# A four-layer block on one core: the first feed-forward's squares move from POOL to ACT, with new instruction orders and PSUM banks

## The reference

```
scores = q k^T + rope(q) rope(k)^T, causal softmax, 16 heads, then W_o      # attention
h = bitlinear(x, w_fc) + gate * (x @ v.T @ fast_b.T @ u.T)                  # first feed-forward
r = maximum(h, 0);  out = bitlinear(r * r, w_proj)
z = x @ W_in; conv; p_w = exp(..); sums = cumsum(p_w * cos / sin(phi)); silu; W_out   # mixer
h = relu(x @ W1 + b1);  out = h @ W2 + b2                                   # second feed-forward
```

## Time and profile before

| | |
|---|---|
| median of 3 runs | 1388.17 us (1387.15 to 1388.91) |
| the profiled execution | 1383.91 us |
| its span | 1382.1 us |
| mean granted clock of TensorE | 0.946 of full speed |
| batches' fc stage (first rectifier to last), of batches 1 to 7 | from 268.7, 437.1, 589.2, 743.7, 890.6, 1048.4, 1185.4 us |

### The profile page before, as it was taken

How to read it: one execution, slowest core, us unless ns; L and a number is a source line. 1 busy time by engine, 2 the same in 40 slices (tenths; PEclk the granted TensorE clock), 3 DMA queues, 4 the chain that set the end, 5 groups by cost and what they waited for, 6 DMA issues and landing times.

```text
span 1382.1 us, 23204 instructions
## 1 busy us (share of the span) xinstructions
PE 1194.7 (86%) x8060; PEld 775.0 (56%) x8060; DVE 1103.5 (80%) x2259; ACT 1054.4 (76%) x2111; POOL 346.8 (25%) x317
## 2 busy tenths in 40 slices
PE   4788995889899989899899999999999998782867
PEld 2575663466556755566656765675655765451434
DVE  2694278999688888989798998899799988988930
ACT  4575699868967998699967989698959887547532
POOL 2953202520133203221134101530133101401021
PEclk9799997999999999999999999999999999896879
DMA  7511341315133104512334131613252131013000
GB/s 235 123 25 36 85 132 41 101 37 140 47 77 90 34 19 145 123 31 54 111 78 98 24 110 39 145 24 96 69 105 57 24 125 31 30 51 105 16 16 16
DMA packets 72084, 101.65 MB, mean 74 GB/s; under 512 B 10640, under 2 KB 44064, under 8 KB 71968
## 3 DMA queue, kind: packets, MB, share of 16 engines
q1 hardware_dynamic: 71968, 100.16, 27.7%
HBM read 74.44 MB, written 25.69 MB: 72 GB/s over the span
## 4 chain that ended last, share of the span: by engine, by line
PE 37%; ACT 23%; DVE 22%; issue 9%; POOL 5%; DMA 2%; SPq 1%; DVEq 0%; POOLq 0%; ACTq 0%
PE ps L885 12%; PE ps L894 10%; DVE work L1526 7%; PE ps L968 4%; ACT work L1213 4%; ACT xnd L1156 3%; DVE work L1449 3%; PE ps L986 3%; ACT work L1220 3%; PE ps L1053 2%; PE ps L960 2%; DVE work L1517 2%; ACT work L1280 2%; POOL later_norms L764 2%; DVE work L1535 2%
## 5 line engine op out<-in xcount | busy, mean ns | idle before, releaser
L1526 DVE TENSOR_TENSOR_SCAN work<-work 128x512 f32<-128x512 f32 x256 | 318.5, 1278 | 38.5 <-ACT work L1280 35.7
L1213 ACT ACTIVATE work<-work 128x384 f32<-128x384 f32 (+3 forms) x512 | 266.4, 564 | 46.0 <-DVE work L1449 45.1
L764 POOL TENSOR_TENSOR later_norms<-later_norms,singles 128x2 f32<-128x2 f32 x112 | 100.8, 903 | 689.4 <-ACT xnd L1156 387.0
L1449 DVE CUSTOM_DVE_ANT_0 work<-ps,work 128x384 f32<-128x384 f32 (+3 forms) x512 | 223.6, 484 | 49.7 <-PE ps L960 47.3
L968 PE MATMUL ps<-ident,work 128*128 128x128 f32 x1280 | 198.9, 280 | 26.8 <-ACT work L1213 21.1
L968 PEld LDWEIGHTS ps<-ident,work 128*128 128x128 f32 x1280 | 149.7, 144 | 76.9 <-issue 51.2
L1220 ACT COPY work<-ps 128x512 f32<-128x512 f32 x300 | 172.0, 580 | 0.4 <-PE ps L968 0.2
L1535 DVE TENSOR_TENSOR work<-work 128x1024 f32<-128x1024 f32 x128 | 162.4, 1269 | 5.1 <-DVEq L1373 0.2
L960 PE MATMUL ps<-work 96*128 96x384 bf16 (+3 forms) x512 | 123.1, 307 | 10.9 <-DMA work<-scratch 8.3
L894 PE MATMUL ps<-wpr,hid 128*128 128x256 f32 x512 | 119.7, 393 | 10.4 <-POOL hid L784 10.4
L894 PE MATMUL ps<-wf,hid 128*128 128x256 f32 x512 | 119.3, 395 | 4.4 <-ACT hid L1296 3.6
(11 more groups left out here) (177 smaller groups left out, 1934.9 us busy)
## 6 DMA issues: line engine op xcount, KB each, us to landing
work<-values SPq DMA_DIRECT2D x64, 256.0 KB, 3.5
work<-ratios SPq DMA_DIRECT2D x64, 256.0 KB, 3.1
scratch<-work SPq DMA_DIRECT2D x32, 384.0 KB, 4.7
work<-scratch SPq DMA_DIRECT2D x64, 192.0 KB, 3.9
work<-scratch SPq DMA_DIRECT2D x64, 128.0 KB, 4.2
x_in<-x SPq DMA_DIRECT2D x8, 512.0 KB, 7.0
work<-scratch SPq DMA_DIRECT2D x64, 64.0 KB, 4.4
values<-work SPq DMA_DIRECT2D x16, 256.0 KB, 2.4
```

Of the source, the lines that this page charges most:

```text
L764: g_.tensor_tensor(rstds[chain][:, tokens], spreads[chain][:, tokens], power[:, tokens], ALU.pow).then_inc(*rstd.one)
L1213: i = s_.activation(part_of, part_of, ACT.Exp, scale=-1.0, bias=nmax[:, row:row + 1])
L1449: i = v_.tensor_tensor_reduce(sc[:, n % 4, at:at + nk], out_of(b, name)[:, at:at + nk], base_of(qt), -SCORE_SCALE, BIG, ALU.add, ALU.min, ...
L1526: v_.tensor_tensor_scan(ring[:, at, m, :], pwr[:, slot, :], ring[:, at, m, :], 0.0, ALU.mult, ALU.add).then_inc(*scanned.one)
```

## The change

ACT takes the squares, one tile behind its rectifier: after rectifying tile n it squares tile n-1, and after the last one both 6 and 7. POOL's item is gone. The signals are the same ones: the square waits for the rectifier's drained signal and gives `hid_sq`.

```diff
     "act": "ystats fstats fystats zstats oystats gstats gystats centre norm ... fc znorm ...",
-    "pool": "stats q k ystats fstats fc fystats zstats oystats gstats gystats gsum ternary tables late",
+    "pool": "stats q k ystats fstats fystats zstats oystats gstats gystats gsum ternary tables late",
...
@@ POOL
-                if item == "fc":
-                    is_drained(pool, b, f"fc{n}")
-                    g_.tensor_tensor(hid[:, n, :], hid[:, n, :], hid[:, n, :], ALU.mult).then_inc(*hid_sq.one)
...
@@ ACT
                     is_filled(act, b, f"fc{n}")
                     s_.activation(hid[:, n, :], out_of(b, f"fc{n}"), ACT.Relu, bias=zero[:, 0:1]
                                   ).then_inc(*drains(b, f"fc{n}"))
+                    for g in (n - 1, n) if n == HC - 1 else (n - 1,) if n else ():
+                        is_drained(act, b, f"fc{g}")
+                        s_.activation(hid[:, g, :], hid[:, g, :], ACT.Square).then_inc(*hid_sq.one)
...
@@ MERGE, all five strings, and BANKS: replaced. The first line of PE's:
-        "a2 p a4 p a3 p2 a p a p a27 p a3 p a4 p a26 p a p a11 p2 a13 p a p a7 p a19 d a2 d2 a4 d6 a3 d a9 d a2 "
+        "a8 p2 a6 p4 a58 p2 a2 p2 a p3 a12 p a15 p a2 p a19 d a2 d9 a3 d a5 d a6 d a2 d2 a13 d a5 d3 a6 d a5 d "
```

More of the change, by code:

```diff
@@ L174 @@
     "pe":
[10 rows of a table removed]
-    "act":
[15 rows of a table removed]
-    "dve":
[12 rows of a table removed]
[10 rows of a table added]
+    "act":
[14 rows of a table added]
+    "dve":
[12 rows of a table added]
     "pool":
-        "a p a4 p4 a4 d2 a3 d15 a4 d2 a3 d16 a7 d18 a d2 a d a2 d a3 d18 a d4 a5 d a d17 a d4 a3 d2 a3 d20 a7 d22 "
-        "a2 d34 p4",
[2 rows of a table added]
     "sp":
-        "a13 d2 a m4 d3 m13 a7 d3 m2 d m6 d m5 a3 m a2 m2 d m d a2 d3 m4 d m d m8 a3 m a2 m3 d2 a2 d2 m4 d2 m4 d "
-        "m5 a m a4 m3 d2 a2 d2 m4 d2 m6 d m5 a3 m a2 d m d a2 d4 m8 d m5 a2 m a3 m2 d m d a2 d2 m4 d2 m5 d m7 d m "
-        "d4 m4 d2 m13 d4",
[3 rows of a table added]
 }
 BANKS = """
-0123450123450132450132450132401534025430243502435124035241324512435214302154321042310234120345201342
@@ L226 @@
-0352430152431502674315607423516074235160742310546372051364253041625301764520376512750261754206152765
-4306153143405413025140365241064735106423514206351435120647351206437512064315042675140263542310643201
-3674103675146021546270516742503614570321673417023672146210356274130754137217267672054371620543715204
-3715204372470163457123406752346503742653071243061753672601536123065241653425145342731532417365402164
-5106754106237514062713450627467146702134567213456712345076123457103625413240652134025617306134270534
@@ L231 @@
-6754203752340715243712540672471562047512463720134572630517263405172065341720653406517240651740625173
-4506241735604723105742130752341065302176375401741645067541602576405170165307165326017365412763570256
-4710265473210546731246053124312640531264035712640532714562703146724036743126034571632470562752740652
-4602653746507314620436710432760134520714635016257306241536213651730462517304516270541267054167253014
-6725036210735612075316450312476052465740237064372160327106316034516304125364207641205436105736412057
@@ L236 @@
-612340576123057612430576123457623104576210453762104537621045
+0123450123450134250134250134201532045203420532405124305241024512405214035214052345203542053421530425
+3415234015230145672301465723014657203145720341705624175036470615370416523462135476251764205741062751
+6375640123670246137042167542306417230651726530172651726304517236107425361042576021456731504365104635
+1423051624056237052634072536024175602341750312547301531247603152743561273045230630512734605124730512
+4730521473051423574620371654371253647213452607145615201462543026573257013562751637215672165302761504
@@ new lines @@
+3201374201563724015246370152407152407631524572631547321567430215673402561342051463254351673562401674
+2410367210367250623570165206471062457106472135460371326507132465071436250714362145307214215307415320
+7645310726435176024136217042761054732604237143632716437163402164327147643170613740657142305647125703
+6125703612405617324017562401240715624071562430715642013647513720176051365270341642573140653431604531
+0543671520731625470126507215674023514603725407216547203157253761540327603152476032547036254307563214
@@ L237 @@
+5602753160732651736215340217365403645230642504326103564130510352710532607512034621057632516324507163
+254701632547163254071632547063245710632471065324710635247106
 """
```

## The result

The changed kernel takes 1390.28 us in the median of 12 runs (1389.13 to 1391.93); the kernel before, on the same chip, 1387.14 us. The ratio is 1.003, with a 95% interval of 1.0021 to 1.004: slower by 0.3%, some 4 us. The forecast was 6 us faster. The time lies inside the range, the sign is wrong.

A forecast was written before the change was run, and what follows sets the result against it. PE was taken as nearest to the bound, 93% busy in the middle, no engine filling the span. Terms -4.9 - 3.5 - 4.0 + 7.0 + 1.3 - 2.0 = -6.1 us, from 1388.17 to 1382.1 us; range 1369 to 1397.

The forecast's parts named there:

- batch 7's fproj: Batch 7's fc stage: without POOL's squares fproj can start at 1198.0, not 1202.93, 4.9 us earlier.
- batch 1's fproj: Batch 1's fc stage: squares end at 284.7 in place of 288.35; taken as 3.5 us earlier.
- middle, POOL's squares gone: Batches 2 to 6: DVE gains 8 us without POOL's squares, half of it on the path, 4 us (0 to 13).
- middle, ACT's cost: Batches 2 to 6: 40 squares put 23.6 us on ACT; between nothing and 14.5 us shown, 7 us taken.
- tables, with start and loads: The start's gain of 2 us and the two added table loads' cost of 1.3 us, together -0.7.
- the rest of the tables: Five orders and all banks differ over the whole middle; not priced, 6 us allowed either way.
- the two loads: ACT has 43 table loads in place of 41, 1.28 us each; half of 2.6 us shown, 1.3 us cost.
- all stayed in the fc stages: Batches 2 to 6: if ACT's squares all stayed in the fc stages, 14.5 us would show.
- ACT becomes the bound beside attention: Rival, 0.26: squares delay exps and transposes; all 23.6 us and both table loads show, +11.8, 1400 us.
- The squares are hidden in full: Rival, 0.18: ACT's idle time takes all the middle's squares, the 7 us fall away, -13.1, 1375 us.
- Gain and cost cancel: Rival, 0.16: about 14 of 26 us show, or the new order loses 6 us elsewhere; within 2.8 us of 1388.17.
- the start: Program start: DVE's constants' operation meets less of POOL's subtraction; 2 us gained of PE's 3.4 idle (0 to 3.4).

The follow-up runs named there:

- old_order_act: The kernel before with its orders and banks kept and all squares moved from POOL to ACT; ratio 1.0009 to the kernel before.
- new_order_pool: The changed kernel's orders and banks with the squares left on POOL; 21.5 us slower than the kernel before.
- experiment 3: Kernel before's orders, each POOL square replaced by two constant writes to the tile, without reading SBUF; ratio 0.9875 to the kernel before, 1366.37 us.

## Why the prediction was wrong

By its steps, in us, with what the runs put in their place. There are two ways from the kernel before to the kernel after, and they give the steps different sizes: move the squares in the old tables and then change the tables, or change the tables first and then move the squares.

```
                              taken    squares moved first    tables changed first
batch 7's fproj               -4.9     -5.0                   -4.2
batch 1's fproj               -3.5     -3.7                   -1.2
middle, POOL's squares gone   -4.0     -7.4                   -13.0
middle, ACT's cost            +7.0     +16.6                  +6.0
the move as a whole           -5.4     +1.2 (medians)         -17.3 (medians)
tables, with start and loads  -0.7     +2.9                   +21.5
sum                           -6.1     +4.2 (2.9 to 5.6)      +4.2
```
Batch 7's step is the change of the time from its first fc product to its first fproj product. Batch 1's is that from the end of its last fc tile to fproj: 7.9 us before, 4.2 in old_order_act, 4.1 in new_order_pool, 2.9 after. These steps come from single executions, and they don't add up exactly to the lines that come from medians.

**The failed step is the price of the middle: "I take the middle, 7 us" for the squares on ACT, and nothing for "the rest of the tables" beside it, as if each could be priced without the other.** Measured from the old tables without squares, squares on ACT and new tables together cost the middle 18.8 us (-7.4 to +11.4), where the prediction had 7.0, and 1.3 for the two loads. In the old tables the squares are 16.6 of it and the tables 2.2; in the new ones the tables are 12.8 and the squares 6.0. So 7 us for ACT was right only in tables that have the room, and such tables are not free: 17.0 us over the whole program without squares, far outside the 6 us allowed. The one fact behind both is in the fc stages. The prediction read that ACT had 9 us there in five stages; its bound of 14.5 us for "all stayed in the fc stages" was near for the old tables, and even that was passed. It expected the new order to find the room, which it did, and had no term for what the room costs. That "no stall in this trace" could be tied to the tables was true, but that gives no reason to put them at zero.

**The gain from POOL's squares was too small too**, 4.0 for 7.4 us in the old tables and 13.0 in the new: the squares cost DVE 21 us of busy time in all (1103.5 to 1082.4 in old_order_act), where the prediction's pieces summed to 14 (in the new tables it is 22: 1100.8 with squares on POOL, 1078.7 without). That the meeting with DVE is the main price of squares on POOL was right, as experiment 3 shows. 21 us over 64 squares are 0.33 us each. By the rule of the Trainium skill that the prediction weighed (SBUF — State Buffer, "Who interferes with whom") a square that meets a two-input DVE instruction holds it in full, which would be 1.03 us each if every square met one; the rows stay well under that. The prediction put its sum under that rule 3.7 us lower, at -9.8; by its own pieces that is too much. PE gives batch 7's last tile at 1195.75, so with a rectifier and two squares behind it fproj couldn't start before 1197.6, 0.4 us ahead of the 1198.0 that it had.

**The rivals.** "ACT becomes the bound beside attention" is what happens in the old tables, where 16.6 us of the middle's squares show; in the kernel after it isn't, since all 64 squares cost 8 us there, and its +11.8 was too large. "The squares are hidden in full" is excluded in both sets of tables, by 22 and 8 us. "Gain and cost cancel" is what old_order_act does (1.0009). The kernel after is 4.2 us slower by the ratio, 1.4 beyond that rival's 2.8. (Its 1390.28 us lies within 2.8 of the 1388.17 that the rival names, but the kernel before measured 1387.14 beside it.) It comes nearest to that rival's second condition, a new order that loses elsewhere.

**The tables** stayed within the allowed 6 us only with the squares on ACT (+2.9), and there by luck: as the difference of a first half that gains 5.5 and a second that loses 8.5. Without squares they cost 17.0 us, with squares on POOL 21.5. The one effect that was read from them, the start, happened at its place and was of no worth. The constants' operation takes 1.13 us and PE's wait of 3.43 us is gone; but when PE has done the same work, at 132 us, the kernel after is level with the kernel before (0.0). Its lead of 2.0 us at b0 S0 lies ahead of that place, at 48.6 us. (The +6.5 at b1 S0 is order: the new tables have PE do batch 0's last fc tiles and first projection ahead of batch 1's scores.)

**The table load**, where the prediction had weighed a page: in the chain of batch 1, the last square ends at 291.55 and the timeline has
```profile
291.56 1.28 ACT L1209 ACT_TABLE_LOAD   x1
292.86 1.33 ACT L1209 ACTIVATE work<-work 128x512 f32<-128x512 f32 x2
```
No drain of 1380 ns stands ahead of it, and the load takes 1283 ns as in the earlier trace rows. So the term by the Trainium skill's page (ScalarE: Activation LUTs, "What ACT_TABLE_LOAD costs") would have been too large. What the two added loads cost the program was not measured apart.

## What to carry to other kernels

When work moves to an engine with idle time, ask what that idle time waits for. Only idle time that lies between the moved work's producer and its consumer is room; here an engine at 83% over the stretch was at 93% where the work had to go. A table of orders can make such room (12.7 us idle in place of 3.9 in these stages), but look for what it pays.

Where orders and an engine's assignment change together, cross them and leave the work out once. Four runs showed that the same squares on ACT cost 22 us in one set of tables and 8 in the other, and that the tables cost 3, 17 or 21 us by where the squares are. A single before and after shows only +4, and a list of separate terms can't hold it. The best place depends on the tables too: in the old ones, squares on ACT at the ends alone gained 0.5% and everywhere nothing; in the new ones the ends alone were 0.6% slower than everywhere.

When orders differ, compare progress where an engine has done the same work, not at a named item: that item may only have been moved.

## What was not expected of the hardware

A POOL multiplication of 128 x 512 and two POOL memsets of the same tile take the same time (1074 ns in the median and 2 x 535 in the mean), and the first costs the kernel 21 us over 64 tiles, the second about 4: the price of work on POOL was in its reads of SBUF beside DVE. Two waits of PE, of 2.63 and 2.55 us, went with 10.2 us at a granted clock of 0.50, and in that stretch of 68.4 us the same matmuls took 4.4 us longer, beside 5.0 us more idle time. A Square on ACT from SBUF to SBUF took 624 ns in the median for 512 columns and moved the queue by 0.52, below the 687 and 0.59 on the line between the norm's 256 columns and the sine's 1024.
